# Two buffers for each gathered row slot, and relation products in two column halves of PE

## What is computed

```python
edge_index = jnp.stack([src, dst])
h = jnp.maximum(_layernorm(x, axis=-1), 0.0)
x = x + _L0_gnn_ref(h, ...)                    # two sums over edges with dense products
h = jnp.maximum(_layernorm(x, axis=-1), 0.0)
x = x + _L1_gnn_ref(h, L1_gnn_weight, src, dst, edge_type_16)
h = jnp.maximum(_layernorm(x, axis=-1), 0.0)
x = x + _L2_gnn_ref(h, ...)                    # three attention layers (GAT)
h = jnp.maximum(_layernorm(x, axis=-1), 0.0)
x = x + _L3_gnn_ref(h, ...)                    # two means over edges with batch norm

def _L1_gnn_ref(feat, weight, src, dst, etypes):
    h_src = feat[src]
    for r in range(num_rels):                  # 16 relations
        mask = etypes == r
        msg = msg + h_src * mask[:, None].astype(feat.dtype) @ weight[r]
    return jax.ops.segment_sum(msg, dst, num_segments=feat.shape[0])
```

## Time and profile before

| | us |
|---|---|
| median of 3 runs | 2144.19 |
| lowest and highest of them | 2142.64, 2149.27 |
| the profiled execution | 2166.85 |
| its span, first to last instruction | 2165.1 |
| granted clock of PE in it, mean | 0.937 |
| busy in the span: PE, DVE, ACT, POOL | 1718.9, 1494.2, 1130.6, 902.7 |

### The profile page before, as it was taken

The page is one execution under the profiler, slowest core; times in us unless marked ns, Lnnn a source line. Parts: engine busy times, 40 slices in busy tenths (PEclk is TensorE's granted clock), DMA queues, the critical chain, the costliest instruction groups (busy, mean ns, idle before and its releaser), DMA issues. The chain is left out here.

```text
span 2165.1 us, 36951 instructions
## 1 busy us (share of the span) xinstructions
PE 1718.9 (79%) x9927; PEld 872.9 (40%) x9928; DVE 1494.2 (69%) x4067; ACT 1130.6 (52%) x2244; POOL 902.7 (42%) x828
## 2 busy tenths in 40 slices
PE   2777776883588888888878888869998998899786
PEld 0222222551244433444434434455545453544254
DVE  6999997425466565665566656578886887788855
ACT  6777776212233333333333433338885887788521
POOL 1000000005666666666666666415553554455500
PEclk9999999996799999999998989979999999999898
DMA  6000000102111111111111111130000000000000
GB/s 175 0 0 0 0 0 8 66 1 63 31 32 29 30 30 29 29 30 31 30 33 30 29 29 30 31 97 1 1 1 1 1 1 1 1 1 1 15 1 16
DMA packets 29633, 50.74 MB, mean 23 GB/s; under 512 B 12820, under 2 KB 13826, under 8 KB 29054
## 3 DMA queue, kind: packets, MB, share of 16 engines
q0 software_dynamic: 17664, 18.12, 4.9%
q1 hardware_dynamic: 11890, 31.59, 4.7%
HBM read 36.58 MB, written 7.39 MB: 20 GB/s over the span
## 5 line engine op out<-in xcount | busy, mean ns | idle before, releaser
L943 POOL DMA_INDIRECT adj<-h_table,l_idx x544 | 559.2, 1028 | 315.8 <-issue 147.1
L1133 DVE TENSOR_SCALAR adj<-adj,node_key 125x1024 f16<-125x1024 f16 x825 | 374.1, 496 | 356.8 <-PE psum L1078 174.3
L1078 PE MATMUL psum<-adj,x_sb 125*128 125x512 f16 x1650 | 435.3, 403 | 160.7 <-DVE adj L1133 137.8
L1643 POOL TENSOR_TENSOR gat_ring<-gat_ring,adj 125x750 f32<-125x750 f32 (+2 forms) x225 | 311.3, 1385 | 263.8 <-ACT gat_ring L1697 261.7
L1538 DVE SCALAR_TENSOR_TENSOR gat_ring<-x_sb,gat_node,psum 125x750 f32<-125x750 f32 (+2 forms) x375 | 317.9, 861 | 60.8 <-PE psum L1774 26.4
L1006 ACT ACTIVATE l_z<-psum 128x320 f32<-128x320 f32 x204 | 89.2, 437 | 478.7 <-remote 258.6
L1078 PEld LDWEIGHTS psum<-adj,x_sb 125*128 125x128 f16 x1650 | 159.2, 102 | 371.5 <-DVE adj L1133 184.2
L393 PE MATMUL psum<-col_hot,src_hot 128*128 128x500 bf16 x808 | 205.7, 376 | 110.1 <-DVE src_hot L322 88.9
L1771 PE MATMUL psum<-gat_ring,gat_hx 125*65 125x500 f32 (+1 forms) x500 | 244.2, 578 | 17.8 <-DVE gat_ring L1549 9.5
L319 DVE TENSOR_SCALAR col_hot<-iota_h,c_tab 128x500 bf16<-128x500 f16 x808 | 227.7, 346 | 25.0 <-PE psum L393 20.5
L1694 ACT ACTIVATE gat_ring<-gat_ring,gat_node 125x750 f32<-125x750 f32 (+2 forms) x225 | 182.2, 810 | 61.0 <-DVE gat_ring L1538 59.1
(11 more groups left out here) (259 smaller groups left out, 2264.7 us busy)
## 6 DMA issues: line engine op xcount, KB each, us to landing
adj<-h_table,l_idx POOLq DMA_INDIRECT x544
adj<-key_table SPq DMA_DIRECT2D x33, 250.0 KB
adj<-adj SPq DMA_DIRECT2D x3, 1662.5 KB
adj_saved<-adj SPq DMA_DIRECT2D x1, 3840.3 KB
adj<-adj_saved SPq DMA_DIRECT2D x5, 688.2 KB
x_sb<-in_x SPq DMA_DIRECT2D x1, 781.2 KB
x_saved<-x_sb SPq DMA_DIRECT2D x1, 781.2 KB
out<-x_sb SPq DMA_DIRECT2D x5, 156.2 KB
```

The source lines that it names most:

```text
L943: pool.indirect_dma_start(out=to[:, t, :], out_offset=None, in_=table[:, :], in_offset=bass.IndirectOffsetOnAxis(ap=index[:, t:t + 1], axi ...
L1078: last = pe.matmul(psum[:, PAIR[half] + t, :], h_parts[:, k, :], select[0:P, k % SELECTS, t * GE:(t + 1) * GE], start=(k == 0), stop=(k == ...
L1133: v.tensor_scalar(select[0:P, k % SELECTS, :], keys, node_key[:, k:k + 1], None, ALU.is_equal).then_inc(s_sel, 1)
L1643: pool.tensor_tensor(slot, slot, adj[:, k, cols(c)], ALU.mult).then_inc(s["weight_ready"], 1)
```

## The change

It has five parts.

1. Each fetched slot has two buffers: `got` is now a pair, one for even and one for odd turns, with a semaphore each. The wait ahead of the gathers of turn j is for PE's use of the rows of turn j - 2, and there is none for turn 1.
2. The 16 output products go to two column halves of PE: even relations add up in PSUM partitions 0 to 63, odd ones in 64 to 127. PARTS is changed, so that each part has an even number. DVE adds both halves to aggT, the second behind the first: two adds for each window.
3. The room for the second buffers: `d_tab` and `type_tab` lie in one table that is stored to DRAM (tab_store, 627 KB) while the edge structures are built, and is read back by SP at the start of the relational loop, ahead of the keys. DVE waits for it.
4. The way in: the residual is added and the rows are summed chunk by chunk inside layer 0's last block. `add_residual`, its barrier and the reduction at L862 go. ACT's scaling of the weights moves behind the copies. POOL copies one set of indices, starts the first eight gathers and copies the rest of the indices after them.
5. In layer 2 ACT runs one small exponential right after the square root.

```diff
--- before.py
+++ after.py
@@ -146,7 +144,12 @@
+        tab_store = nc.dram_tensor("tab_store", [128, 3 * G * GT], FP16, kind="Internal").ap()
...
+        tabs = sb("edge_tabs", [128, 3 * G * GT], FP16, build_scope)[:, :]
+        d_tab, type_tab = tabs[:, 0:2 * G * GT].bitcast(FP32), tabs[:, 2 * G * GT:3 * G * GT]
@@ -297,8 +300,10 @@
+                    sp.dma_start(tab_store, tabs).then_inc(s_tabs, 16)
...
+                    sp.wait_ge(s_tabs, 16)
@@ -774,9 +779,14 @@
                     act.activation(stat[:, 1, :], stat[:, 0, :], ACT.Sqrt).then_inc(s_nrm, 1)
...
+            def residual_and_sums(link, tiles):
+                v, xc = nc.vector, x_sb[:, tiles, :]
+                link(v.tensor_tensor(xc, xc, z[:, tiles, :], ALU.add))
+                link(v.tensor_reduce(stat[:, 0, tiles], xc, AX.X, ALU.add))
...
             sage_layer("l0b", h[:, :, :], stack, high, parts, None, z[:, :, :], vec0("L0_b2"), mat("L0_W2l", 2 * D),
-                       False)
-            add_residual(nc, sem("l0_residual"), x_sb, z)
+                       False, after_chunk=residual_and_sums)
@@ -806,10 +816,12 @@
-        got = carve(4 * GT * 2 * D).rearrange("p (g t d) -> p g t d", g=4, t=GT)
+        got_odd = sb("l1_got_odd", [128, 4, GT, 2 * D], FP16, l1_scope)[:, :, :, :]
+        got = carve(4 * GT * 2 * D).rearrange("p (g t d) -> p g t d", g=4, t=GT), got_odd
...
-        dw_tab = hot_space.bitcast(FP32)[:, 0:G * GT]
+        loaded_tabs = hot_space[:, 0:3 * G * GT]
+        dw_tab, type_back = loaded_tabs[:, 0:2 * G * GT].bitcast(FP32), loaded_tabs[:, 2 * G * GT:3 * G * GT]
@@ -841,13 +853,13 @@
-                act.wait_ge(s_rel, 32)
-                act.activation(rel[D:2 * D, :, :], rel[D:2 * D, :, :], ACT.Copy, scale=1.0 / LO_SCALE).then_inc(s_relc, 1)
...
+                act.wait_ge(s_rel, 32)
+                act.activation(rel[D:2 * D, :, :], rel[D:2 * D, :, :], ACT.Copy, scale=1.0 / LO_SCALE).then_inc(s_relc, 1)
@@ -859,7 +871,6 @@
-                link(v.tensor_reduce(stat[:, 0, :], x_sb[:, :, :], AX.X, ALU.add))
@@ -897,7 +908,8 @@
-        s_got = [sem(f"l1_gathered{k}", l1_scope) for k in range(4)]
+        s_got = [[sem(f"l1_gathered{half}_{k}", l1_scope) for k in range(4)] for half in range(2)]
+        s_tabs_in = sem("l1_edge_tabs_in", l1_scope)
@@ -907,7 +919,7 @@
-        PARTS = ((0, 3), (3, 6), (6, 9), (9, 11), (11, 14), (14, R))
+        PARTS = ((0, 4), (4, 6), (6, 10), (10, 12), (12, 14), (14, R))
@@ -922,6 +934,7 @@
+                    sp.dma_start(loaded_tabs, tab_store).then_inc(s_tabs_in, 16)
                     keys(0, 0)
@@ -949,20 +962,22 @@
                         if not static(j, 1):
                             pool.wait_ge(s_ix, j - 1)
                         for k in range(4):
-                            pool.wait_ge(s_z, SIX * (j - 1) + FREED[k])
+                            if not static(j, 1):
+                                pool.wait_ge(s_z, SIX * (j - 2) + FREED[k])
                             pool.sem_inc(s_tick, 1)
-                            gather(got[:, k, :, :], idx[:, half, k * GT:(k + 1) * GT], s_got[k])
+                            gather(got[half][:, k, :, :], idx[:, half, k * GT:(k + 1) * GT], s_got[half][k])
                     pool.tensor_copy(idx[:, 0, :], src_tab[:, 0:4 * GT]).then_inc(s_ix0, 1)
+                    pool.wait_ge(s_ix0, 1)
+                    pool.sem_inc(s_tick, 1)
+                    for k in range(2):
+                        gather(got[0][:, k, :, :], idx[:, 0, k * GT:(k + 1) * GT], s_got[0][k])
                     pool.tensor_copy(idx_first[:, :], src_tab[:, 4 * GT:6 * GT]).then_inc(s_ix0, 1)
                     pool.tensor_copy(idx[:, 1, :], src_tab[:, SIX * GT:(SIX + 4) * GT]).then_inc(s_ix0, 1)
                     pool.wait_ge(s_ix0, 3)
-                    pool.sem_inc(s_tick, 1)
-                    for k in range(2):
-                        gather(got[:, k, :, :], idx[:, 0, k * GT:(k + 1) * GT], s_got[k])
                     gather(pair_pick[:, 0, :, :], idx_first[:, 0:GT], s_first[0])
                     for k in range(2, 4):
-                        gather(got[:, k, :, :], idx[:, 0, k * GT:(k + 1) * GT], s_got[k])
+                        gather(got[0][:, k, :, :], idx[:, 0, k * GT:(k + 1) * GT], s_got[0][k])
                     gather(pair_pick[:, 1, :, :], idx_first[:, GT:2 * GT], s_first[1])
                     fetch(1, 1)
                     with nc.Fori(1, TURNS // 2, engines=[ENG.Pool], head_slot={ENG.Pool: 0}) as q:
@@ -1037,14 +1052,14 @@
                 def _(pe):
-                    def z(j, pos):
+                    def z(j, pos, half):
                         n = SIX * j + pos
...
                         if pos in FETCHED:
-                            pe.wait_ge(s_got[FETCHED[pos]], 16 * GT * (j + 1))
-                            rows = got[:, FETCHED[pos], :, :]
+                            pe.wait_ge(s_got[half][FETCHED[pos]], 8 * GT * (j + 2 - half))
+                            rows = got[half][:, FETCHED[pos], :, :]
                         else:
@@ -1062,11 +1077,12 @@
                             pe.wait_ge(s_zs, SIX * j + SIX)
                             if not (static(j, 0) or static(j, 1)):
-                                pe.wait_ge(s_added, SIX * j - SIX)
+                                pe.wait_ge(s_added, 2 * (SIX * j - SIX))
                         for r in range(lo, hi):
-                            last = pe.matmul(psum[0:D, SUMS[half], 0:SIX * W], rel[:, r, :],
-                                             zs[:, half, r, :, :].rearrange("p a w -> p (a w)"), start=(r == 0),
-                                             stop=(r == R - 1), skip_group_check=True)
+                            side = slice(r % 2 * D, r % 2 * D + D)
+                            last = pe.matmul(psum[side, SUMS[half], 0:SIX * W], rel[:, r, :],
+                                             zs[:, half, r, :, :].rearrange("p a w -> p (a w)"), start=(r < 2),
+                                             stop=(r >= R - 2), skip_group_check=True)
                         if hi == R:
                             last.then_inc(s_sum, 1)
@@ -1139,10 +1155,12 @@
                             dve.wait_ge(s_sum, j + 1)
+                        win = aggT[:, bass.ds(base, W)]
                         if not static(SIX * j + pos, 0):
-                            dve.wait_ge(s_added, SIX * j + pos)
-                        win = aggT[:, bass.ds(base, W)]
+                            dve.wait_ge(s_added, 2 * (SIX * j + pos))
                         v.tensor_tensor(win, win, psum[0:D, SUMS[half], pos * W:(pos + 1) * W], ALU.add).then_inc(s_added, 1)
+                        dve.wait_ge(s_added, 2 * (SIX * j + pos) + 1)
+                        v.tensor_tensor(win, win, psum[D:2 * D, SUMS[half], pos * W:(pos + 1) * W], ALU.add).then_inc(s_added, 1)
@@ -1191,10 +1209,11 @@
-                    link(v.tensor_scalar(dw_tab, d_tab, pass_off[:, 0:1], None, ALU.subtract))
+                    dve.wait_ge(s_tabs_in, 16)
+                    link(v.tensor_scalar(dw_tab, dw_tab, pass_off[:, 0:1], None, ALU.subtract))
...
-                    link(v.scalar_tensor_tensor(dw_tab, dw_tab, 1.0, type_tab, ALU.add, ALU.add))
+                    link(v.scalar_tensor_tensor(dw_tab, dw_tab, 1.0, type_back, ALU.add, ALU.add))
@@ -1669,6 +1688,8 @@
+            act.wait_ge(s["ln_std"], 1)
+            act.activation(stat[:, 0, :], stat[:, 2, :], ACT.Exp, scale=0.0).then_inc(s["exp_begun"], 1)
@@ -1836,14 +1857,6 @@
-def add_residual(nc, s_res, x_sb, z, width=D):
-    with nc.Block() as block:
-        @block.vector
-        def _(dve):
-            nc.vector.tensor_tensor(x_sb[:, :, :], x_sb[:, :, :], z[:, :, 0:width], ALU.add).then_inc(s_res, 1)
-            dve.wait_ge(s_res, 1)
```

16 lines of the change are left out of this document (7 added, 9 removed).

## The result

The changed kernel takes 2438.89 us (median of 4 runs, 2433.72 to 2442.09), the kernel before 2145.64 us in the same comparison. The ratio is 1.134 (95% interval 1.131 to 1.137): 293 us slower. The forecast was 2124 us with a range up to 2250. Even the rival in which the long run shuts the others out named only 2258 us.

A forecast was written before the change was run, and what follows sets the result against it. It took PE's completions reaching others late while POOL issues gathers as the bound. Second buffers -25, halves +6 and way in, tail and exponential together -1 made -20 us, 2144.2 to 2124 us; range 2045 to 2250, its own 2092 to 2149.

The forecast's parts named there:

- the rival in which the long run shuts the others out: Relational loop: a run of 16 gathers keeps the share of 0.61, +109 us, 2258 us in all; chance 0.25.
- What bounds the kernel: Relational loop: no engine is full; while POOL issues gathers, news that PE is done reaches others late; DVE waits 9.1 us a turn.
- The second buffers' term: Relational loop: runs join to 16; DVE's waits as a share of gather time go from 0.44 to 0.40, -25 us.
- the rival on POOL's pace: Relational loop: turns fall to 16 gathers and one restart, 22.9 us for 25.9, so 2056 us; chance 0.15.
- The far end: Run of 36 gathers: DVE's waits over gather time, 0.61, taken as the highest share; +109 us.
- The rival that the gathers have no part: Relational loop: the lateness belongs to something else and second buffers do nothing, 2149 us; chance 0.10.
- The start: First turns of the relational loop: turn 0 is the run of 36 in both kernels, turns 1 and 2 already had long runs.
- Outputs in halves: PE's outputs and DVE's adds in the loop: +0.54 and -0.33 us a turn reach the time, +6 us.
- The way in: Ahead of the loop: residual and sums -3.4, ACT's copies -1.6, tables read back from DRAM +1; sum -4 us.
- The residual's part: Way in: residual and row sums leave the path, 4.2 us, while the last chunk's 0.7 remains: -3.4 us.
- The tail: End of the loop: the last two turns' adds run alone, 12 more at 0.28 us: +3.4 us.
- The exponential: Layer 2: a table load of 1.28 us moves to where ACT may wait anyway, -0.6 us.

## Why the prediction was wrong

- **What bounds the kernel** held. The lateness of PE's completions while POOL gathers was an inference from three wake-ups, and the kernel without gathers bears it out: 18.1 us a turn for 25.9.
- **The second buffers' term was mis-sized, and with its sign.** "Runs of 12 say 0.31, the runs of now 0.44, the run of 36 says 0.61": I took 0.40, a third of the way towards the 0.31. The share was 0.77, so the term was +8.0 us a turn and not -0.8. The step that failed is the choice of the row to lean on. Turns 1 and 2 looked like the nearest case, a run of 12. They came behind the stall of the run of 36, and I take it that this left DVE and PE work to catch up on, as the rival on POOL's pace said against itself; no run tests that. PE's news was late in these turns too, up to 4.7 us. In the steady state length 4 to 8, 8 and 16 gave 7.2, 9.9 and 15.0 us of waits a turn. So the waits grow with the run, by half from 8 to 16. My reading is that the ring of 5 selections bridges a short wait and not a long one; what is shown is that PE then stands (7.33 us in the timeline), that its granted clock is 0.78 of full speed for 0.93 in the steady part, and that a pick took 430 ns for 403.
- **The far end was too near.** I bounded the share by 0.61, since the run of 36 held "also waits for data of the way in". That reads the row the wrong way. At first PE's news came on time in that run: ACT began to copy z at 528.19 and 533.18, each within 0.05 us of the z's end, when PE still waited for gathered rows. The next z ended at 538.49, and ACT woke for it at 557.71, 1.5 us behind the end of the run at 556.24. So the length alone does not say when the lateness sets in, some 25 to 30 us into that run and 2 to 4 us into a steady run of 16; why isn't shown. A bound must come from the worst stretch of a row, not from its mean with the harmless part in it.
- **The rival of the long run** was the true case: DVE's waits over 10 us a turn, ending 2 to 3 us after the run (it had said 1 to 2), with ACT's copies. It had 0.25, and its time of 2258 us was 181 us short. The rival that the gathers have no part, which the Trainium skill's page would give (SBUF — State Buffer, "SBUF: two separate sides"), is out by the 242 us that the kernel without gathers saves.
- **The start** I had as equal, "the run of 36 in both". With no wait for turn 1, and the indices of turn 2 written by then, a run of 56 came, 505.34 to 578.38. PE's first z of turn 1 starts at 545.0 for 566.8 us, since the stall at the end of turn 0 did not come there, but that of turn 2 at 601.8 for 590.3 and that of turn 3 at 636.2 for 612.2: 24 us lost by then. From there to the loop's end (1681.88 and 1410.54) it is 1045.7 us for 798.3, so 247 us more in 31 turns, 8.0 each. Together that is all of the 271 us between the two spans.
- **Outputs in halves.** Predicted were 0.85 us a turn less work for PE and 1.7 more for DVE, of which -0.33 and +0.54 were to reach the time, +6 us in all. The groups over the whole span:

```profile
L1083 PE MATMUL psum<-l_z,l_rel 128*64 128x120 f32 x1088 | 109.9, 304 | 1.2 <-issue 0.9 <-ACT l_z L1021 0.2
L1163 DVE TENSOR_TENSOR l_aggT<-l_aggT,psum 64x20 f32 x204 | 36.3, 178 | 7.0
L1161 DVE TENSOR_TENSOR l_aggT<-l_aggT,psum 64x20 f32 x204 | 34.3, 168 | 21.6 <-issue 4.4 <-PE psum L1083 3.7 <-DVE adj L1137 1.6
```

  Neighbouring halves do overlap: the 1088 records fall from 165.2 to 109.9 us, 1.6 us a turn (to 106.3 us with POOL's waits as before, where the mean clock is 0.934 for 0.937), in the upper half of my bounds (0 to 2.5) and short of the 2x that the Trainium skill allows (TensorEngine Tiling (Array Packing), "Theoretical Speedup"). The second add costs 36.3 + 7.0 = 43.3 us of DVE, 1.3 us a turn. The two comparisons without the long run (0.997 with halves, 0.997 without) put the sum at 0 within some 5 us.
- **The way in.** Predicted -4 us. The steps in the timeline, to be held beside the earlier trace rows:

```profile
486.01 0.29 DVE L785 TENSOR_TENSOR x_sb<-x_sb,l_z 125x128 f32<-125x128 f32 x1
486.33 0.29 DVE L786 TENSOR_REDUCE stat<-x_sb 125x2 f32<-125x128 f32 x1
487.10 2.71 POOL L867 MEMSET l_aggT<- 64x3146 f32 x1 [472.63 <-POOLq L509]
487.14 2.71 DVE L874 TENSOR_SCALAR stat<-stat 125x25 f32<-125x25 f32 x1 [0.52 <-PEq L509]
...
496.05 0.47 ACT L859 ACTIVATE x_sb<-adj 125x320 f16<-125x320 f32 x1 [0.97 <-DVE adj L889]
...
505.34 1.30 POOL L956 DMA_INDIRECT adj<-h_table,l_idx  x1 [0.94 <-POOL l_idx L970]
...
508.25 0.65 DVE L1213 TENSOR_SCALAR adj<-adj,pass_off 128x816 f32<-128x816 f32 x1 [3.68 <-DMA adj<-tab_store]
...
514.56 1.22 PE L1072 MATMUL psum<-adj 128*128 128x320 bf16 x4 [28.91 <-ACT adj L997]
```

  The first gather starts 3.3 us earlier and the first z 2.1 us. The residual's part, for which I had counted 3.4 us, hardly came: DVE's centring (L877) starts at 489.88 for 490.28, since the small instruction ahead of it (L874, L863 before) ends 0.04 and 0.05 us behind the end of POOL's memset in both kernels (at 489.81 and 490.20). Alone an instruction of that form takes 0.18 us (L883); L874 took 2.71. The memset sets this point, and it starts only 0.4 us earlier. The gain came from the term that I had put at 1.6 us: ACT's copies no longer wait for the weights and start at 496.05 for 499.41. What used to release that z was the gathers' DMA; now it is ACT's first one-hot tile, which hangs on the tables: DVE waited 3.68 us for them. So the reload ate a part of the gain, by the wait that was named, at about its predicted size of 1 us: going by the first gather, the rows would have allowed a first z 3.3 us earlier, and it came 2.1 us earlier. The kernel with the way in alone gained 0.3%, 6 us, of which the first z explains 2; the rest has no cause shown.
- **The tail** of 12 more adds cost less than the predicted 3.4 us: a window takes 0.51 us for 0.28, so 12 x 0.23 = 2.8 us.

```profile
1679.53 0.17 DVE L1161 TENSOR_TENSOR l_aggT<-l_aggT,psum 64x20 f32 x1
1679.73 0.18 DVE L1163 TENSOR_TENSOR l_aggT<-l_aggT,psum 64x20 f32 x1
1680.04 0.17 DVE L1161 TENSOR_TENSOR l_aggT<-l_aggT,psum 64x20 f32 x1
```

- **The exponential** gained nothing of its 0.6 us. The table load now stands at 1697.43, but from the loop's end (L1231 at 1681.88, L1212 at 1410.54 in the kernel before) to the next table load at 2310.40 and 2039.03 it is 628.52 and 628.49 us.

## What to carry to other kernels

Before two waits are taken away that seem to cost an engine its time, ask what its work does to the others while it runs without a pause: here POOL's waits cut its gathers into short runs, which let everybody else go on, and a second buffer, which had room for the data, joined them to one long run. When the cost of a longer run is wanted and only short ones are in the trace, do not take the share from turns just behind a stall; look at how much slack (here a ring of 5 selections and two banks of z) the waiting engines have, and let the bound be what happens once it is used up. And put the cheap question first: a kernel without the disputed transfers showed at once that they cost 242 us, where they looked like idle time of somebody else.
